# The causal mask in the maxima: from mask matmuls on TensorE to a fused add-and-maximum on VectorE

## What is computed

```python
scores = jnp.einsum('bhqd,bhkd->bhqk', qc, k) * scale
causal_mask = k_pos[None, :] > q_pos[:, None]
scores = jnp.where(causal_mask[None, None], -jnp.inf, scores)
m = jnp.max(scores, axis=-1, keepdims=True)
p = jax.nn.softmax(scores - m, axis=-1)
oc = jnp.einsum('bhqk,bhkd->bhqd', p, v)
```

## Time and profile before

| | |
|---|---|
| median of 3 runs | 597.0 us (596.98 to 597.73) |
| profiled execution | 598.1 us |
| its span, first to last instruction | 596.4 us |
| TensorE busy | 531.0 us (89%) |
| VectorE busy | 452.0 us (76%) |
| ScalarE busy | 363.7 us (61%) |
| GpSimd busy | 142.6 us (24%) |
| mean granted TensorE clock | 0.961 |
| L982, the maxima | 320 instructions, 324.6 us busy |
| L1244, score matmuls | 640, 110.5 us busy |
| L1251, mask matmuls | 512, 35.8 us busy |

### The profile page before, as it was taken

One profiled execution on the slowest core, in us unless ns is written; L12 is line 12 of the kernel. 1 busy time (PEld: TensorE's weight loads), 2 busy tenths in 40 slices (PEclk: granted clock), 3 DMA queues, 4 the chain that ended last, 5 costly groups with the idle time before them and its releaser, 6 DMA issues.

```text
span 596.4 us, 12259 instructions
## 1 busy us (share of the span) xinstructions
PE 531.0 (89%) x4393; PEld 202.1 (34%) x4393; DVE 452.0 (76%) x765; ACT 363.7 (61%) x805; POOL 142.6 (24%) x268
## 2 busy tenths in 40 slices
PE   5478898899999999999999999999998999998980
PEld 3233233333323333222222223223224225664460
DVE  4796999999888888886888789779824425767683
ACT  3015666566777666777777776776797884331450
POOL 4623320312203021020101002002013157214744
PEclk9657999999999999999999999999999999999995
DMA  6341000240010511000010010000001012211233
GB/s 155 101 114 51 2 2 29 72 117 28 2 28 2 154 34 29 2 6 24 1 28 2 1 28 2 2 2 2 1 1 36 20 34 56 45 50 40 48 66 92
DMA packets 28875, 22.49 MB, mean 38 GB/s; under 512 B 3528, under 2 KB 28048, under 8 KB 28816
## 3 DMA queue, kind: packets, MB, share of 16 engines
q1 hardware_dynamic: 26848, 18.43, 10.9%
q0 software_dynamic: 1536, 3.15, 3.0%
q10 hardware_dynamic: 432, 0.13, 0.1%
HBM read 8.00 MB, written 4.06 MB: 20 GB/s over the span
## 4 chain that ended last, share of the span: by engine, by line
PE 61%; DVE 20%; ACT 6%; issue 6%; POOL 5%; DMA 2%; POOLq 0%; SPq 0%; DVEq 0%; ACTq 0%
PE ring_ps L1280 20%; PE out_ps L1300 19%; DVE part_max L982 13%; PE score_ps L1244 7%; ACT probs L857 4%; PE score_ps L1390 3%; PE ring_ps L1407 1%; PE score_ps L1280 1%; PE ring_ps L1211 1%; PE ring_ps L1310 1%; PE score_ps L1251 1%; POOL k_stack L797 1%; PE score_ps L1342 1%; POOL k_stack L687 1%; POOL qk_parts L784 1%
## 5 line engine op out<-in xcount | busy, mean ns | idle before, releaser
L982 DVE TENSOR_REDUCE part_max<-score_ps 128x2 f32<-128x1024 f32 (+3 forms) x320 | 324.6, 1060 | 56.7 <-PE score_ps L1244 29.5
L857 ACT ACTIVATE probs<-ring_ps 128x512 f32<-128x512 f32 (+3 forms) x603 | 287.4, 531 | 114.7 <-PE ring_ps L1280 111.8
L1280 PE MATMUL ring_ps<-q_stack,k_stack 64*128 64x512 bf16 (+3 forms) x1206 | 203.3, 351 | 10.7 <-ACT probs L857 7.8
L1300 PE MATMUL out_ps<-probs,v_aug 128*32 128x512 f32 (+3 forms) x1280 | 151.4, 544 | 4.4 <-POOL probs L717 4.1
L1244 PE MATMUL score_ps<-k_stack,q_stack 64*128 64x512 bf16 (+3 forms) x640 | 110.5, 362 | 21.0 <-DVE part_max L982 14.3
L1280 PEld LDWEIGHTS ring_ps<-q_stack,k_stack 64*128 64x128 bf16 x1206 | 53.2, 94 | 133.7 <-ACT probs L857 109.3
L717 POOL TENSOR_SCALAR_AFFINE_SELECT probs<-probs 128x512 f32<-128x512 f32 x64 | 40.7, 636 | 183.8 <-ACT probs L857 183.6
L1244 PEld LDWEIGHTS score_ps<-k_stack,q_stack 64*128 64x128 bf16 x640 | 31.7, 95 | 91.6 <-DVE part_max L982 62.9
L1300 PEld LDWEIGHTS out_ps<-probs,v_aug 128*32 128x32 f32 x1280 | 25.5, 108 | 49.9 <-ACT probs L857 24.3
L784 POOL DMA_INDIRECT qk_parts<-xs_dram,q_stack x30 | 30.6, 1019 | 26.3 <-DVE q_stack L1109 18.5
L1251 PE MATMUL score_ps<-mask_wide,ident_wide 64*128 64x128 bf16 (+1 forms) x512 | 35.8, 222 | 0.0
(11 more groups left out here) (177 smaller groups left out, 405.5 us busy)
## 6 DMA issues: line engine op xcount, KB each, us to landing
q_stack<-qk_parts SPq DMA_DIRECT2D x36, 128.0 KB, 2.5
k_stack<-qk_parts SPq DMA_DIRECT2D x36, 128.0 KB, 2.4
sorted_dram<-q_stack SPq DMA_DIRECT2D x30, 64.0 KB, 1.5
x_sb<-in_L_attn_x_dram SPq DMA_DIRECT2D x4, 256.0 KB, 4.4
w_gu<-n_L_ffn_expert_gate_dram SPq DMA_DIRECT2D x8, 128.0 KB, 2.1
w_gu<-in_L_ffn_expert_up_dram SPq DMA_DIRECT2D x8, 128.0 KB, 2.2
wd<-n_L_ffn_expert_down_dram SPq DMA_DIRECT2D x8, 128.0 KB, 2.3
xs_dram<-qk_f SPq DMA_DIRECT2D x4, 256.0 KB, 2.3
```

The lines of the kernel that those rows point to most:

```text
L857: act.activation(probs[:, u % RING, 0:w], bank(("probs", u))[:, 0:w], ACT.Exp, scale=SCALE).then_inc(probs_ready, 1)
L982: dve.tensor_reduce(out=part_max[:, s % 2, t, 2 * hp:2 * hp + 2, c], in_=score_ps[:, m % 2, :, 0:w], axis=AX.X, op=ALU.max).then_inc(score ...
L1280: last = mm(bank(unit)[:, 0:w], k_stack[half, j // TPB, rows, hh, keys], q_stack[half, B % 2, rows, hh, skip:BLK], start=rows == MAIN, sto ...
L1300: last = mm(out_ps[at:at + 32, skip:BLK], v_aug[:, j, h * VC:h * VC + 32], probs[:, (4 * k + i) % RING, 0:w], start=j == 0, stop=j == TPB ...
```

## The change

In a diagonal job the four mask matmuls go. VectorE's one reduction over both heads becomes two `tensor_tensor_reduce` instructions, one for each head: each adds the mask to the scores, writes the sum back to PSUM, and gives its maximum to `part_max`. Jobs off the diagonal stay as they are. The mask is a tile of 512 bf16 columns, zero but for the triangle in its last 128; it lies in a part of `qk_f` that held the scratch tile of odd blocks, so `rest` now has one copy. The set-up on GpSimd has one clearing less, and `ident_bf` is a tile of its own. The planner books 85 ns less on TensorE and 120 ns more on VectorE for a diagonal job.

```diff
+LOWEST = -3.0e38
@@ make_plan
-            clock["tensor"] += 0.42 * w + 85 * (c == B)
-            slots[m % 2] = clock["vector"] = max(clock["vector"], clock["tensor"] + LATENCY) + 2.08 * w + 64
+            clock["tensor"] += 0.42 * w
+            slots[m % 2] = clock["vector"] = max(clock["vector"], clock["tensor"] + LATENCY) + 2.08 * w + 64 + 120 * (c == B)
...
-        ident_wide = sb("ident_wide", [P, 2 * P], BF16)
-        mask_wide = sb("mask_wide", [P, P + 64], BF16)
-        ident_bf = ident_wide[:, 64:64 + P]
+        ident_bf = sb("ident_bf", [P, P], BF16)
...
+        mask = qk_f[:, 1, 1, 0:BLK // 2].bitcast(BF16)
...
@@ gpsimd
-            pool.memset(mask_wide[:, :], 0.0).then_inc(pool_step, 1)
-            pool.memset(ident_wide[:, :], 0.0).then_inc(pool_step, 1)
+            pool.memset(mask, 0.0).then_inc(pool_step, 1)
...
-            pool.affine_select(out=mask_wide[:, :], in_=mask_wide[:, :], compare_op=ALU.is_ge, fill=MASKED,
-                               base=0, pattern=[[-1, P + 64]], channel_multiplier=1).then_inc(pool_step, 1)
+            square = mask[:, BLK - P:BLK]
+            pool.affine_select(out=square, in_=square, compare_op=ALU.is_ge, fill=MASKED,
+                               base=0, pattern=[[-1, P]], channel_multiplier=1).then_inc(pool_step, 1)
...
@@ vector
-                    rest = qk_f[:, side, b % 2, :]
+                    rest = qk_f[:, side, 0, :]
...
-                    dve.tensor_reduce(out=part_max[:, s % 2, t, 2 * hp:2 * hp + 2, c], in_=score_ps[:, m % 2, :, 0:w],
-                                      axis=AX.X, op=ALU.max).then_inc(scores_read, 1)
+                    if c < B:
+                        dve.tensor_reduce(out=part_max[:, s % 2, t, 2 * hp:2 * hp + 2, c], in_=score_ps[:, m % 2, :, 0:w],
+                                          axis=AX.X, op=ALU.max).then_inc(scores_read, 1)
+                    else:
+                        if m == 0:
+                            dve.wait_ge(pool_step, 5)
+                        for x in range(2):
+                            last = dve.tensor_tensor_reduce(
+                                out=score_ps[:, m % 2, x, 0:w], in0=score_ps[:, m % 2, x, 0:w], in1=mask[:, BLK - w:BLK], scale=1.0,
+                                scalar=LOWEST, op0=ALU.add, op1=ALU.max, accum_out=part_max[:, s % 2, t, 2 * hp + x, c:c + 1])
+                        last.then_inc(scores_read, 1)
@@ tensor
-                                  k_stack[half, c, MAIN, hh, 0:w], start=True, stop=c < B)
-                    if c == B:
-
-                        for y, skip in enumerate((0, 64)):
-                            for x, half in enumerate(HALVES):
-                                at = 64 * (x - y)
-                                last = mm(score_ps[:, m % 2, x, w - P + skip:w], ident_wide[half, 64 + at:64 + at + P],
-                                          mask_wide[half, at + skip:at + P], start=False, stop=y == 1)
+                                  k_stack[half, c, MAIN, hh, 0:w], start=True, stop=True)
```

More of the change, by code:

```diff
@@ L666, in _ @@
             pool.memset(ident[:, :], 0.0).then_inc(pool_step, 1)
-            pool.memset(mask_wide[:, :], 0.0).then_inc(pool_step, 1)
-            pool.memset(ident_wide[:, :], 0.0).then_inc(pool_step, 1)
-            pool.wait_ge(pool_step, 3)
+            pool.memset(mask, 0.0).then_inc(pool_step, 1)
+            pool.wait_ge(pool_step, 2)
             pool.affine_select(out=ident[:, :], in_=ident[:, :], compare_op=ALU.not_equal, fill=1.0,
                                base=0, pattern=[[-1, P]], channel_multiplier=1).then_inc(pool_step, 1)
-            pool.wait_ge(pool_step, 4)
-            pool.tensor_copy(ident_bf, ident[:, :]).then_inc(pool_step, 1)
-            pool.affine_select(out=mask_wide[:, :], in_=mask_wide[:, :], compare_op=ALU.is_ge, fill=MASKED,
-                               base=0, pattern=[[-1, P + 64]], channel_multiplier=1).then_inc(pool_step, 1)
+            pool.wait_ge(pool_step, 3)
+            pool.tensor_copy(ident_bf[:, :], ident[:, :]).then_inc(pool_step, 1)
+            square = mask[:, BLK - P:BLK]
+            pool.affine_select(out=square, in_=square, compare_op=ALU.is_ge, fill=MASKED,
+                               base=0, pattern=[[-1, P]], channel_multiplier=1).then_inc(pool_step, 1)
             for i, bias in enumerate((bv, bo)):
@@ L678, in _ @@
                                ).then_inc(bias_vo_loaded, 16)
-            pool.wait_ge(pool_step, 6)
+            pool.wait_ge(pool_step, 5)
             for b in range(NB):
@@ L695, in _ @@
                 pool.memset(hot_before[:, a + w, :], 0.0).then_inc(consts_ready, 1)
-            steps = 6
+            steps = 5
             pool.memset(minus_half[:, :], -0.5).then_inc(pool_step, 1)
@@ L1165, in _ @@
             mm, turn = pe.matmul, pe.transpose
-            pe.wait_ge(pool_step, 6)
+            pe.wait_ge(pool_step, 5)
             pe.wait_ge(qk_loaded, 32)
@@ L1259, in _ @@
                         last = mm(bank(it)[0:4 * PARTS, t * P:(t + 1) * P],
-                                  max_parts[:, s % 2, t, :, :, :].rearrange("p x a j -> p (x a j)"), ident_bf,
+                                  max_parts[:, s % 2, t, :, :, :].rearrange("p x a j -> p (x a j)"), ident_bf[:, :],
                                   start=True, stop=True)
```

## The result

The changed kernel takes 605.15 us (median; 603.71 to 608.0) against 597.37 us for the kernel before in the same comparison: a ratio of 1.0117, 95% interval 1.009 to 1.0145. It is slower; the forecast was 594.8 us. A second comparison, among the experiments, gives 1.0094 (1.0065 to 1.0123).

What follows compares the result with a forecast made beforehand. VectorE's maxima were taken to set the pace to about 150 us, TensorE after. +1.7 early, -4.3 and +0.4 late gave -2.2 us from 598.1 profiled, or 594.8 us on the median scale; range of 8 in 10: 589.5 to 606.

Steps and rivals of the forecast that it cites:

- The extra of a fused pair, e: VectorE's extra fixed cost per diagonal job for two fused operations instead of one reduction: 0.16 us, ends 0.07 and 0.62.
- The first rival: On VectorE each fused operation has its own spaced readout, e = 0.245: slower, 601.2 us; chance 0.22.
- half rate: Fourth rival: VectorE's fused operation streams at half throughput, far slower, some 645 us; chance 0.04.
- three signs against e: Separate short instructions behind fused ones, successor at 1.4 us or later, score jobs' waits for `part_max` above 14.3 us.
- I put 9.5 us of the 13.7 as absorbed: Up to 150 us, VectorE's idle time takes 9.5 of 11.2 us extra work (ends 5 and 13), leaving +1.7 us.
- From 150 to 435 us this is 58 x 0.088 = 5.1 us. I take 85% of it: TensorE sets the pace late, so 58 diagonal jobs without mask matmuls save 4.3 us; ends 5.1 and 1.
- the sign that the prediction named for a wrong saving: TensorE's gap behind a diagonal job falls from 0.31 to 0.23 us, yet waits for `probs` grow by as much.
- I add 0.4 us: From 150 us on, VectorE's 9.3 us extra hides in 45.7 us of idle, but for the two score slots: +0.4 us.
- The order (0 +- 2): The planner's new costs move score jobs against `probs` in TensorE's order: 0 +- 2 us.
- The bound of 14.3 us: Limit on what order can win or lose: score jobs' waits for VectorE, 5.4 + 4.7 + 4.2 us in three stretches.
- The third: No change: e near 0.2, or TensorE's saving hidden behind the exponentials (1 instead of 4.3 us): 598.1 us; chance 0.17.
- The second, the clock: Without mask matmuls TensorE is less busy and its clock may stay low until 60 us: +5, 599.8 us; chance 0.08.

Runs made afterwards that it cites:

- A second comparison: The changed kernel itself, run again beside the kernel before as partner of a run with added TensorE work: 604.69 us, ratio 1.0094.
- the kernel without masks: The kernel before with its mask matmuls left out and nothing put in their place: 597.23 us, ratio 0.9962.
- the change with the old order: The changed kernel with the planner's costs of before, so that TensorE's order is that of before: 605.6 us, ratio 1.012.
- its traced repeat: A repeat profiled execution of the changed kernel that starts like the kernel before: 606.67 us.

## Why the prediction was wrong, step by step

**The extra of a fused pair, e: right.** Taken as 0.16; measured 0.145 by VectorE's busy time, and 1.29 us from pair to pair where 1.32 was named as the sign. VectorE's busy time rose by 18.6 us (15 to 25). The rule of the Trainium skill ("VectorE: DVE Perf Modes", section "Two Vector instructions with no wait between them") holds as to the count: the readout is an instruction with a row of its own. The first rival's price for it, 0.08 us of spacing each, does not, since readout and next operation start together. Nor did half rate come: the 512-column operation takes 0.716 us. Two of the three signs against e came all the same, instructions of their own and waits of 22.1 us; a late VectorE makes such waits whatever e is.

**"I put 9.5 us of the 13.7 as absorbed": the early step that failed.** Only 4.6 us of idle time were filled. Up to the sixth copy VectorE has 9.4 us more work, and 9.4 - 4.6 = 4.8 us is what the copy comes later, where +1.7 was forecast. I took idle time as room. It is room only where VectorE could have had its next job sooner, and in the two stretches shown TensorE's list holds the score job back. The lower end of this term, 5, which stood in the range and not in the sum, was the right value.

**"From 150 to 435 us this is 58 x 0.088 = 5.1 us. I take 85% of it": the late step that failed.** The saving is 0.9 us by the trace of the kernel without masks, near the lower end of 1. The gap of 0.31 us did fall to 0.23, and the waits for `probs` grew, which is the sign that the prediction named for a wrong saving. The mistake was in the first reading: a TensorE busy 273 of 285 us was taken for the one that sets the pace. Its second group of `probs` matmuls stood in the record as 0.96 us of busy time where the first takes 0.61, and the difference was a wait for banks; the view of waits had 91.3 us of it on the weight loads, and it is the view that the 4.2 us of the earlier trace rows comes from. I passed over that row and looked at the idle time of the matmuls (0.20 us in the earlier trace rows) instead.

**"I add 0.4 us" for the late slots: too small.** From the sixth copy to the fifteenth the change with the old order takes 1.0 us more, although the missing masks give 0.9: the fused operations cost 1.9 there.

**The order (0 +- 2): right in size**, 1.0008 by itself, but not in the way it was to help: the work that it carries into the late stretch found no free room there (+2.4 us). The bound of 14.3 us on it counted matmuls alone; the weight loads of the score jobs waited another 11.8 + 23.1 + 28.0 us for VectorE in the three stretches.

**The sum.** Early +4.8 where +1.7 stood, late +1.0 where -3.9 stood (-4.3 + 0.4): +5.8 instead of -2.2, with the fault 3.1 us early and 4.9 us late. This is the change in the old order; behind the fifteenth copy it wins 0.8 us back, so its span is 5.0 us longer. The two comparisons of the change have 5.6 us (1.0094) and 7.0 us (1.0117), and its traced repeat has 8.5 us more span (+5.5 and +3.4 in the table). So some 5 us are accounted for; the rest, in which the clock and the slower start are mixed, is not resolved.

**The rivals.** The first gave 601.2 us by a readout that came, but not at the price named. The third had the right mechanism for the late part (TensorE's saving behind the exponentials) but kept 9.5 us absorbed, and so came out at no change. The slow result was the two low ends together, 5 absorbed and 1 saved, and no rival stood for that: 70 x 0.16 - 5 - 1 + 0.4 is +5.6 us, 602.6 us on the scale of the medians. The measured 605.2 us lies inside the range of 8 in 10, 589.5 to 606, but by luck: the upper end was put there for the dear readout. The second, the clock, occurred in part: it stayed at 0.50 to 53 us and fell again, and what that cost is open. Its sign, a clock of 0.5 after 50 us, could not have told, since the kernel before has one too.

## What to carry to other kernels

A matrix engine that is busy 96% of a stretch need not set its pace: compare equal groups of its matmuls, read what its weight loads wait for, and see whether the period of the loop changes with its content; here 2.82 us stayed 2.82 with no masks, with them and with twice as many. Idle time of the engine that is to take over work is not all room: where that engine waits for something that stands in another engine's list, the extra moves the wait instead of filling it; here half of the early extra showed. And before work is moved from one engine to another, ask if it is needed: the maxima without any mask were the only change that was faster.

## What the runs showed of the hardware that was not expected

The readout of a fused operation's maximum overlaps the next operation: fused operations of 512, 384 and 128 columns follow each other after 0.65, 0.52 and 0.25 us, with a readout row of 0.14 us for each.

At the start matmuls can take twice as long while the granted clock of the record is 1.00. The same four matmuls, in the profiled executions of before and of after (the granted clock is 1.00 in every 2 us from 14 to 20 us in both):

```profile
13.69 1.95 PE L1211 MATMUL ring_ps<-xT,wT 128*128 128x512 f32 x4 [0.78 <-ACT xT L833]
```

```profile
15.16 3.69 PE L1220 MATMUL ring_ps<-xT,wT 128*128 128x512 f32 x4 [0.78 <-ACT xT L833]
```

In the second of these job 0 starts no later (22.33 us, against 22.23); it is VectorE's first maximum that comes later, at 23.39 us against 22.64 in the repeat. What decides between the two was not tried.
